# The first norm's output turned by DMA transposes instead of TensorE, in a two-layer graph network

## The reference: what is computed

```
h = max(layernorm(x), 0)
x = x + Attention(h, adj)         # q, k, v = h@Wq+bq, h@Wk+bk, h@Wv+bv; 16 heads of 32; softmax; @Wo + bo
h = max(layernorm(x), 0)
x = x + Graph(h, adj)             # relu(h@wq @ (h@wk).T) * (adj != 0), softmax over axis 1, @ (h@weight)
```

## Time and profile before

| | |
|---|---|
| median of 3 runs | 1844.52 us (1842.23 to 1845.1) |
| the profiled execution | 1843.87 us |
| its span in the profile | 1842.1 us |
| PE busy | 96% of the span |
| DVE busy | 84% |
| ACT busy | 59% |
| mean granted TensorE clock | 0.991 of full speed |

### The profile page before, as it was taken

The page is one execution under the profiler, slowest core; times in us unless marked ns, Lnnn a source line. Parts: engine busy times, 40 slices in busy tenths (PEclk is TensorE's granted clock), DMA queues, the critical chain, the costliest instruction groups (busy, mean ns, idle before and its releaser), DMA issues.

```text
span 1842.1 us, 53154 instructions
## 1 busy us (share of the span) xinstructions
PE 1762.0 (96%) x16817; PEld 1410.2 (77%) x16817; DVE 1547.1 (84%) x4586; ACT 1094.3 (59%) x2445; POOL 511.3 (28%) x1286
## 2 busy tenths in 40 slices
PE   3889999999999999999999999999999999999996
PEld 2567878787888887787878788887778787877873
DVE  5778888888888888888888888888888888888883
ACT  2456665666656666666566666656666666666651
POOL 2023232233222233322223322323332222333111
PEclk9999999999999999999999999999999999999998
DMA  3422222322222232222232222223222222222220
GB/s 118 153 57 65 71 85 82 89 74 71 68 76 83 83 90 71 70 64 82 83 87 75 71 71 73 83 82 91 71 72 62 82 83 86 79 70 71 63 63 23
DMA packets 195401, 142.48 MB, mean 77 GB/s; under 512 B 36000, under 2 KB 167072, under 8 KB 195360
## 3 DMA queue, kind: packets, MB, share of 16 engines
q1 hardware_dynamic: 178224, 108.93, 20.8%
q10 hardware_dynamic: 17136, 33.03, 5.6%
HBM read 57.94 MB, written 16.78 MB: 41 GB/s over the span
## 4 chain that ended last, share of the span: by engine, by line
PE 81%; DVE 9%; issue 5%; ACT 2%; SPq 2%; DMA 1%; POOL 0%; ACTq 0%; DVEq 0%; POOLq 0%
PE ring L380 58%; PE turned L445 10%; PE score L430 5%; PE pv L463 3%; DVE val L920 2%; PE ring L498 2%; SPq L333 2%; DVE probs L828 2%; PE pv L465 1%; DVE work L888 1%; DVE probs_t_lo L836 1%; ACT val L657 1%; ACT stage L650 1%; PE ring L530 1%; DVE tops L761 0%
## 5 line engine op out<-in xcount | busy, mean ns | idle before, releaser
L619 ACT ACTIVATE probs_t_hi<-turned 128x512 f16<-128x512 f32 x512 | 305.2, 596 | 319.7 <-PE turned L445 318.7
L609 ACT ACTIVATE probs<-probs,least 128x256 f32<-128x256 f32 x1024 | 461.8, 505 | 6.7 <-DVE least L828 6.6
L828 DVE CUSTOM_DVE_ANT_0 probs<-score,far,undo_score 128x256 f32<-128x256 f32 x1024 | 449.7, 476 | 11.8 <-DVE far L1012 9.4
L1123 POOL TENSOR_TENSOR heads_out<-o_sum,o_rcp 128x64 f32<-128x64 f32 x512 | 146.9, 308 | 1043.3 <-DVE o_sum L849 1034.0
L836 DVE TENSOR_TENSOR probs_t_lo<-turned,probs_t_hi 128x512 f16<-128x512 f32 x512 | 349.4, 682 | 28.6 <-ACT probs_t_hi L619 24.9
L445 PE MATMUL turned<-ident,probs 128*128 128x128 f32 x2048 | 308.7, 273 | 6.2 <-ACT probs L609 6.1
L445 PEld LDWEIGHTS turned<-ident,probs 128*128 128x128 f32 x2048 | 246.5, 141 | 49.1 <-ACT probs L609 7.9
L430 PE MATMUL score<-stack 128*128 128x256 f16 x1024 | 196.2, 273 | 3.9 <-DMA stack<-stage 3.9
L463 PE MATMUL pv<-val,probs_t_hi 128*128 128x65 f16 x2048 | 184.4, 191 | 4.6 <-DVE probs_t_lo L836 4.2
L465 PE MATMUL pv<-val,probs_t_lo 128*128 128x33 f16 x2048 | 178.0, 179 | 0.0
L463 PEld LDWEIGHTS pv<-val,probs_t_hi 128*128 128x128 f16 x2048 | 157.5, 97 | 11.9 <-DVE probs_t_lo L836 6.0
(11 more groups left out here) (163 smaller groups left out, 4236.0 us busy)
## 6 DMA issues: line engine op xcount, KB each, us to landing
stack<-stage SPq DMA_DIRECT2D x2048, 32.0 KB, 1.9
xin<-x_dram ACTq DMA_DIRECT2D x32, 512.0 KB, 3.9
out_dram<-xo SPq DMA_DIRECT2D x32, 512.0 KB, 2.9
xa<-x_dram ACTq DMA_DIRECT2D x31, 512.0 KB, 3.7
adj_in<-adj_dram SPq DMA_DIRECT2D x32, 256.0 KB, 2.8
adjt_in<-adj_t_dram SPq DMA_DIRECT2D x32, 256.0 KB, 2.9
wq_raw<-wq_dram SPq DMA_DIRECT2D x2, 512.0 KB, 6.4
wk_raw<-wk_dram SPq DMA_DIRECT2D x2, 512.0 KB, 8.1
```

The lines of the kernel that those rows point to most:

```text
L609: last = nc.scalar.activation(probs[:, u % 2, q, :], probs[:, u % 2, q, :], ACT.Exp, bias=least[:, u % 2, q:q + 1], scale=-1.0)
L619: nc.scalar.activation(pH[:, u % 2, :, :], turned[u % 2][:].rearrange("p (k n) -> p k n", k=QT), ACT.Copy).then_inc(hi["p"], 1)
L828: last = nc.vector.tensor_tensor_reduce(out=probs[:, u % 2, q, :], in0=score[u % 2][:, q * NODES:(q + 1) * NODES], in1=far[:, q, :], scale ...
L1123: last = nc.gpsimd.tensor_tensor(dst, o_sum[:, pair % 2, q:q + 3:2, :], o_rcp[:, pair % 2, q:q + 3:2].unsqueeze(2).broadcast_to([P, 2, HEAD]),
```

## The change: what it does

The eight transposes of `h1` on PE, their two ACT and two DVE instructions on PSUM, and the tiles `h1_0` and `h1_1` of the ring are gone. In their place:

- ACT rounds relu(xa) to f16 for all 256 nodes in one instruction of 128x1024 (`first_high`), at the end of step 15, for the graph two further on than the body's. The target is `hw`, a tile that the second layer's `hw0` and `hw1` use at another time of the body.
- DVE makes the lo halves from `xa` in SBUF, one instruction of 128x512 in step 0 and one in step 1 of the next body (`first_low`).
- SP issues two DMA transposes (`transpose_h1`), each of the hi and lo halves of 128 nodes (128 partitions x 1024 f16, 256 KB), into `h1`. They stand behind the stack of qk2 and ahead of the store and the stack of qk3, and wait until `qk3` and `v1` of the graph before have been read out of `h1`.
- `qk` and `v` on PE now wait for the transposes' DMAs (`h1_in`), and so does ACT ahead of the hi half of `hw0`, which overwrites what they read.
- The ring has 19 tiles instead of 21, so each tile's bank changes; `ot0` is put by hand into the bank of `av1`.

```
-    ["h1_0", "h1_1", "g0"],
+    ["g0"],
...
+BANK["ot0"] = BANK["av1"]
...
+XA_STEP, SCALE_STEP = 6, 6
+HIGH1_STEP, LOW1_STEPS = 15, (0, 1)
...
+            def transpose_h1(b):
+                if started(b - 1):
+                    sp.wait_ge(mm["qk"], count(b - 1, 4, 3))
+                    sp.wait_ge(mm["v"], count(b - 1, 2, 1))
+                for q in range(QT):
+                    sp.wait_ge(lo["h1"], count(b, QT, q))
+                    settle(sp, sp_settled)
+                    sp.dma_start_transpose(
+                        h1[:, :, :, q * P:(q + 1) * P].rearrange("p h d n -> p (h d) n"),
+                        hw[:, q, :, :].rearrange("p h d -> p (h d)")).then_inc(h1_in, 16)
...
                 if cur:
                     stack_heads(2, t)
+                if nxt:
+                    transpose_h1(n)
                 if cur and not prev:
                     load_late(2)
...
-                if name.startswith("h1"):
-                    pe.wait_ge(normed[0], count(b, 2, k))
-                    for d in range(KT):
-                        last = nc.tensor.transpose(dst[:, d * P:(d + 1) * P],
-                                                   xa[:, k, d * P:(d + 1) * P], ident[:])
-                    last.then_inc(mm["h1"], 1)
...
                 elif name.startswith("qk"):
-                    pe.wait_ge(lo["h1"], count(b, 2, 1))
+                    pe.wait_ge(h1_in, count(b, QT, QT - 1) * 16)
...
                 elif name.startswith("hw"):
                     act.wait_ge(mm["hw"], count(b, 2, k))
-                    if started(b - 1):
+                    if isinstance(b, int) and b + 2 >= BATCH:
                         act.wait_ge(mm["av"], count(b - 1, 2, 1))
+                    else:
+                        act.wait_ge(h1_in, count(b + 2, QT, QT - 1) * 16)
...
+            def first_high(b):
+                act.wait_ge(normed[0], count(b, QT, QT - 1))
+                if started(b - 3):
+                    act.wait_ge(mm["av"], count(b - 3, 2, 1))
+                nc.scalar.activation(hwH, xa[:], ACT.Relu).then_inc(hi["h1"], 1)
...
+                    if s == HIGH1_STEP and later:
+                        first_high(n + 1)
...
+            def first_low(q, b):
+                dve.wait_ge(hi["h1"], count(b, 1, 0))
+                relu_low(hwL[:, q, :], xa[:, q, :], hwH[:, q, :], lo["h1"])
...
+                    if s in LOW1_STEPS and nxt:
+                        first_low(LOW1_STEPS.index(s), n)
```

More of the change, by code:

```diff
@@ L61 @@
 ORDER = [name for step in DENSE for name in step if not name.endswith("b")]
-assert len(ORDER) % RING == 0 and len(DENSE) == HEADS
+assert len(DENSE) == HEADS
 BANK = {tile(name): i % RING for i, name in enumerate(ORDER)}
+BANK["ot0"] = BANK["av1"]
 ROLE = {"v1": 0, "ot1": -1, "qk2": 0, "wo0": -1, "wo1": -1, "qk3": 0, "h2_0": -1, "h2_1": -1,
-        "hw0": -1, "g0": -1, "g1": -1, "h1_0": 1, "h1_1": 1, "hw1": -1, "qk0": 1, "al": -1,
+        "hw0": -1, "g0": -1, "g1": -1, "hw1": -1, "qk0": 1, "al": -1,
         "av0": -1, "av1": -1, "qk1": 1, "ot0": 0, "v0": 1}
@@ L107, in bank_before @@
     while True:
-        at -= RING
+        at -= 1
         if at < 0:
@@ L111, in bank_before @@
         other = ORDER[at]
+        if BANK[tile(other)] != BANK[tile(name)]:
+            continue
         graph = t + shift + ROLE[other]
@@ L175, in two_layers @@
         keep = sb("keep", [P, QT, NODES], bf16)
-        h1H = sb("h1_hi", [P, KT, NODES], f16)
-        h1L = sb("h1_lo", [P, KT, NODES], f16)
+        h1 = sb("h1", [P, 2, KT, NODES], f16)
+        h1H, h1L = h1[:, 0, :, :], h1[:, 1, :, :]
         stage = sb("stage", [P, 2, 4, NODES], f16)
@@ L194, in two_layers @@
         gL = sb("g_lo", [P, KT, NODES], f16)
-        hwH = sb("hw_hi", [P, QT, DIM], f16)
-        hwL = sb("hw_lo", [P, QT, DIM], f16)
+        hw = sb("hw", [P, QT, 2, DIM], f16)
+        hwH, hwL = hw[:, :, 0, :], hw[:, :, 1, :]
         eH = sb("e_hi", [P, QT, NODES], f16)
@@ L222, in two_layers @@
         stored = sem("stored")
+        h1_in = sem("h1_in")
         small_in = sem("small_in")
@@ L234, in two_layers @@
         mm = {n: sem(f"mm_{n}") for n in
-              ("h1", "qk", "v", "score", "turn", "pv", "ot", "wo", "h2", "g", "al", "hw", "av")}
+              ("qk", "v", "score", "turn", "pv", "ot", "wo", "h2", "g", "al", "hw", "av")}
         hi = {n: sem(f"hi_{n}") for n in ("h1", "qk", "v", "p", "ot", "h2", "g", "e", "hw")}
@@ L252, in two_layers @@
         nstep = [sem("nstep1"), sem("nstep2")]
-        dve_settled, pool_settled = sem("dve_settled"), sem("pool_settled")
+        dve_settled, pool_settled, sp_settled = (
+            sem("dve_settled"), sem("pool_settled"), sem("sp_settled"))
         x1_ok, keep_ok, far_next_ok = sem("x1_ok"), sem("keep_ok"), sem("far_next_ok")
@@ L493, in signal @@
                         last.then_inc(mm[kind], 1)
[L495 to L501 removed]
+                if name.startswith("h2"):
                     pe.wait_ge(normed[1], count(b, 2, k))
@@ L585, in body @@
                             merge(SPARE.index(tile(name)), *bank_before(name, t))
-                    if nxt and not cur and s == step_of("h1_1"):
+                    if nxt and not cur and s == SCALE_STEP:
                         find_scale(0, 2, pv)
@@ L626, in dense_high @@
                 tok = slice(k * P, (k + 1) * P)
-                if name.startswith("h1"):
-                    act.wait_ge(mm["h1"], count(b, 2, k))
-                    if started(b - 1):
[L630 to L635, removed]
+                if name.startswith("h2"):
                     act.wait_ge(mm["h2"], count(b, 2, k))
@@ L741, in body @@
                             split_high(c)
-                    if "h1_1" in DENSE[s] and later:
-                        act.wait_ge(mm["h1"], count(n, 2, 1))
+                    if s == HIGH1_STEP and later:
+                        first_high(n + 1)
+                    if s == XA_STEP and later:
+                        act.wait_ge(lo["h1"], count(n, QT, QT - 1))
                         act.dma_start(xa[:], x_v[n + 1, :, :, :]).then_inc(xa_in, 16)
             act.wait_ge(const_ok, 2)
+            first_high(0)
             sweep(act, body)
```

2 lines of the change are left out of this document (removed).

## The result

| | before | changed |
|---|---|---|
| median of 4 runs | 1844.08 us (1842.23 to 1845.1) | 1867.15 us (1864.69 to 1870.08) |
| span of the profiled execution | 1842.1 us | 1865.8 us |
| PE busy | 96% | 93% |
| DVE busy | 84% | 83% |
| ACT busy | 59% | 59% |

The change makes the kernel slower: ratio 1.0127, 95% interval 1.0109 to 1.0144. PE has less to do and the run is longer.

What follows compares the result with a forecast made beforehand. PE, busy 96%, was taken to wait ahead of g0 for DVE's h_lo, its transposes filling that hole. Conversion 21.7 us, removal -3.1 and start +4 gave +22.6 us: 1866 us predicted, range 1842 to 1888.

Steps and rivals of the forecast that it cites:

- The removal: Steps 5 and 6: taking PE's eight transposes away gains only 0.1 us a body, since g0 still waits for h_lo.
- the hole: Step 6, ahead of g0: PE's time between val freeing a bank and h_lo being there, made by DVE's chain.
- Rival (1): Steps 5 and 6: PE's own pace holds g0, so the removal gains up to 1.43 us a body; 1826; chance 0.11.
- ACT's conversion: Steps 15 to 1: conversion holds ACT 1.05 us against 0.41 slack, so turn of step 1 starts 0.70 us later per body.
- rival (2): Steps 15 to 1: ACT's conversion is hidden, holding ACT for under 0.5 us; 1845 us; chance 0.08.
- DVE's lo halves: Steps 0 and 1: two lo halves of 0.64 us each, costed at nothing; without cover up to 0.6 us each.
- rival (4): Steps 0 and 1: DVE's lo halves cost as well, up to 0.6 us a body more; 1884; chance 0.08.
- The DMA transposes: SP's queue after v1: 2.5 us each, within the 13.1 us available, so costing nothing in a full body.
- Rival (3): DMA transposes beyond 6 us each make hw0 and qk0 wait in each body; about 2140 at 10 us each; chance 0.13.
- The start: Graph 0 and body 0: +1.5 us at the first product and +3 from the later load of wo; together +4.
- The sum: Whole run: 31 bodies x 0.70, 31 x -0.1 and start +4 give +22.6 us.

Runs made afterwards that it cites:

- hole_filled: Changed kernel with eight float32 128x128 identity transposes, results unused, put back on PE in step 6 ahead of g0's wait; 1861.87 us.
- lo_last: Changed kernel with g0's first half reordered: eight products with the hi half of h2 first, only then the wait for the lo halves; 1835.77 us.
- best_filled: The kernel best with eight unused identity transposes put back on PE ahead of g0; 1811.28 us.
- act_alone: Kernel before, with only ACT's 128x1024 conversion of xa added at the end of step 15, into a tile nobody reads; 1860.87 us.
- late_high: Changed kernel with ACT's conversion moved to the end of step 2 of the next body and DVE's lo halves to steps 3 and 4; 1840.11 us.
- twice: Changed kernel with each body's two DMA transposes issued a second time into an unread tile, waits raised to all four; 1872.74 us.
- load_first: Changed kernel with body 0's load of wo and w1 issued ahead of the DMA transposes instead of behind them; 1863.75 us.
- best: Changed kernel with the edits of late_high, lo_last and load_first, and second_normalise moved from step 5 to step 4; 1787.45 us.

## Why the prediction was right

**The removal.** Right: PE idles 1.46 us where 1.3 were forecast, released by `h_lo`, and the time from `turn` of step 5 to `g0` did not move. The term of 0.10 us was too hopeful; measured is 0.00. It was read from the 0.11 us between `h_lo`'s end and `g0`'s weight load, which was no slack: in the changed kernel, with nothing in between, `g0` follows `h_lo` no sooner (0.15 us against 0.14). hole_filled shows that the transposes were free, lo_last and best_filled that this is so only while the hole is there. Rival (1) falls with hole_filled.

**ACT's conversion.** Right in place and cause, shown by act_alone and late_high; rival (2) falls. The size was taken 0.12 too large and lay outside my bounds of 0.62 to 0.79: `turn` of step 1 comes 0.58 us later than before, not 0.70, and PE idles 0.77 us ahead of it, not 0.9. The conversion took 1.06 us and held ACT for 0.95, where the weight split's row had 1.14 and I took 1.05 from its starts; the measured 0.95 is just under my lower bound of 0.97. Another 0.06 us, which the prediction did not have, is lost from step 1 to step 2 (2.72 us against 2.66). It lies in `turn` itself, 0.66 us instead of 0.60: before, its weight load starts at 935.55, 0.11 us ahead of it, and in the changed kernel with it, at 950.19, since both wait for `probs`.

**DVE's lo halves.** Costed at nothing. In the profile DVE has no gap from 949.38 to beyond `wo0`'s read-out, so its slack is used up, but PE waited for none of it. act_alone has no such halves and almost the same body, with the same 0.66 us for `turn` of step 1, so they cost 0.02 us at most, and rival (4) falls.

**The DMA transposes.** Forecast at 2.5 us each on the queue, measured 1.28, and 3.3 to land, near the lower bound of 2.8. Right in the conclusion, shown by `twice`; the price on the queue was twice too high, which the 13.1 us hid. Rival (3) falls. With it falls the estimate from the Trainium skill ("VectorE: DVE Perf Modes", The three transpose paths), 1309 ns a block taken one after another, 10.5 us for eight: from issue to landing eight blocks took 3.3 us.

**The start.** Forecast +4. Ahead of the load at 183.44 the run has lost 4.8 us, of which some 1.3 would be the 0.67 of two bodies; 3.5 are left. That is close to the forecast, but a start varies by some 2 us (hole_filled), so it is weakly measured; load_first shows that a part of it is the load of `wo`. The first product runs at 25.70 instead of 25.37, so graph 0's transposes cost 0.3 and not 1.5.

**The sum.** Forecast 22.6 us, measured 23.07 in the medians. A full body was forecast at 0.70 - 0.10 = 0.60 us longer and is 0.67 longer, of which 0.58 and 0.06 are found at the seam and 0.03 stay unplaced. That the sum is within 0.5 us is in part luck: the conversion was 0.12 too dear, the removal 0.10 too hopeful, and the 0.06 and 0.03 were not foreseen; the first error covers the rest but for 0.07 us a body.

## What to carry to other kernels

That an engine is busy for 96% of the time does not make it the one to relieve. Look up what releases the instruction behind the work that is to go; if it is another engine's chain, the work fills a hole, and taking it away is worth nothing until something else is put there. And a conversion moved to an engine with 40% idle time costs what it holds that engine less the slack of that one place (here 0.95 - 0.41 us, measured 0.58): find a step in which the engine waits for longer than that, and put it there.

## What the runs showed of the hardware that was not expected

- A DMA transpose of 128 x 1024 f16 from SBUF to SBUF holds SP for 1.28 us, three times a plain issue of 0.4 us, and lands 3.3 us after its issue, where a copy of the same bytes from HBM took 2.8. With 2 MB of loads issued right ahead of them, in body 0 of load_first, two held SP for 5.84 us, where the same two of the changed kernel held it for 3.05; in `best` and best_filled it was 7.09 and 6.16:

```profile
69.04 1.11 SPq L280 DMA_DIRECT2D wo_raw<-wo_dram  x2
70.19 0.98 SPq L280 DMA_DIRECT2D w_raw<-w_dram  x2
71.80 5.84 SPq L351 DMA_TRANSPOSE h<-hw  x2
```

- The 64 transposes add 67584 packets, 1056 each, to the 195401 of before, all of them under 512 B (36000 before, 103584 after).
- DVE's lo half in step 0 took 0.86 us, the same instruction in step 1 0.69. In step 0 GpSimd was in its two additions on 128x512 in SBUF (949.84 to 952.80). Moved to steps 3 and 4 in late_high all 64 took 0.68 to 0.69. That GpSimd's work is the cause is argued from this, not tested by itself; late_high moved other work too.

```profile
950.79 0.86 DVE L909 SCALAR_TENSOR_TENSOR hw<-xa,hw 128x512 f16<-128x512 f32 x1
...
953.01 0.69 DVE L909 SCALAR_TENSOR_TENSOR hw<-xa,hw 128x512 f16<-128x512 f32 x1
```
